# Five stretches of VectorE routing per part instead of three, among the attention slots of a cross-attention and mixture-of-experts kernel

## The reference

```
y = x + attn(layernorm(x), ctx)       # 16 heads of 16, layernorm of q and k per head, softmax over 154 keys
h = layernorm(y)
scores = sigmoid(h @ W_router)        # 8 experts
sel = top_k(scores + bias, 2)         # w = the two scores, divided by their sum
out = y + shared_ffn(h) + sum_k w_k * expert_ffn[sel_k](h)
```

## Time and profile before

| what | value |
|---|---|
| median of 3 runs | 616.65 us (615.98 to 617.1) |
| the profiled execution, its own time | 616.69 us |
| span of its trace | 614.9 us |
| busy: TensorE, VectorE, ScalarE, GpSimd | 524.6, 345.0, 239.4, 244.2 us |
| the attention slots in the trace | 52.8 to 301.6 us |
| the shared expert; the experts | to about 380 us; 404 us to the end |

### The profile page before, as it was taken

One profiled execution on the slowest core, in us unless ns is written; L12 is line 12 of the kernel. 1 busy time (PEld: TensorE's weight loads), 2 busy tenths in 40 slices (PEclk: granted clock), 3 DMA queues, 4 the chain that ended last, 5 costly groups with the idle time before them and its releaser, 6 DMA issues.

```text
span 614.9 us, 10970 instructions
## 1 busy us (share of the span) xinstructions
PE 524.6 (85%) x2868; PEld 311.6 (51%) x2869; DVE 345.0 (56%) x1040; ACT 239.4 (39%) x468; POOL 244.2 (40%) x218
## 2 busy tenths in 40 slices
PE   4746899998798977988689999479999999999990
PEld 3633245544354444433265555157676766767670
DVE  5875556777747757635556663225555555555550
ACT  0256888776647834654324111012222222222220
POOL 5353411120011533442114475605656547564644
PEclk9956999998969967988879999879999999999996
DMA  8903701110011211121054384225656547565634
GB/s 276 354 30 132 212 18 36 45 61 18 17 36 35 88 52 53 60 80 52 19 190 150 105 275 155 91 73 80 116 84 105 99 80 118 86 110 88 103 55 48
DMA packets 41685, 59.75 MB, mean 97 GB/s; under 512 B 6703, under 2 KB 32047, under 8 KB 41168
## 3 DMA queue, kind: packets, MB, share of 16 engines
q0 software_dynamic: 16256, 26.49, 21.2%
q1 hardware_dynamic: 25392, 32.82, 17.9%
HBM read 31.76 MB, written 29.52 MB: 100 GB/s over the span
## 4 chain that ended last, share of the span: by engine, by line
PE 67%; DVE 13%; DMA 7%; issue 5%; ACT 4%; POOL 2%; POOLq 1%; SPq 1%; DVEq 0%; ACTq 0%
PE bankS L955 13%; PE bankS L971 8%; PE bankV L866 7%; PE bankR L741 7%; PE bankS L1006 6%; PE bankQ L741 5%; DMA out<-VR,attn 5%; PE bankV L870 3%; PE bankS L841 2%; PE bankS L853 2%; PE bankR L748 1%; ACT attn L622 1%; PE bankS L1022 1%; PE bankD L944 1%; PE bankQ L962 1%
## 5 line engine op out<-in xcount | busy, mean ns | idle before, releaser
L530 POOL DMA_INDIRECT out<-VR,attn x72 | 111.1, 1544 | 101.2 <-DVE VR L1417 57.0
L955 PE MATMUL bankS<-experts,scores_in 128*128 x288 | 105.0, 498 | 2.1 <-issue 1.1
L473 POOL DMA_INDIRECT sorted_rows<-XR,route x64 | 63.3, 989 | 107.1 <-PE bankD L872 48.6
L622 ACT ACTIVATE attn<-bankS,bias 128x512 f32<-128x512 f32 x128 | 81.1, 680 | 24.3 <-PE bankS L841 24.2
L971 PE MATMUL bankS<-experts,scores_in 96*128 x288 | 74.3, 380 | 0.0
L866 PE MATMUL bankV<-attn,VS 128*32 128x512 f32 x256 | 69.0, 664 | 1.7 <-DVE OTT L1192 1.7
L955 PEld LDWEIGHTS bankS<-experts,scores_in 128*128 128x128 f32 x288 | 52.6, 193 | 34.2 <-issue 9.7
L868 PE MATMUL bankD<-attn,ON 128*32 128x512 f32 x256 | 68.9, 664 | 0.0
L705 ACT ACTIVATE scores_in<-bankS 128x192 f32<-128x192 f32 x72 | 23.8, 330 | 110.8 <-PE bankS L955 110.8
L409 POOL DMA_DIRECT2D x_in<-in_xT x13 | 9.6, 736 | 127.3 <-PE bankQ L741 126.3
L1402 DVE TENSOR_TENSOR scores_in<-scores_in,bankS 128x192 f32<-128x192 f32 x72 | 25.5, 354 | 52.5 <-ACT scores_in L705 52.1
(11 more groups left out here) (252 smaller groups left out, 916.9 us busy)
## 6 DMA issues: line engine op xcount, KB each, us to landing
VS<-sorted_rows SPq DMA_DIRECT2D x72, 130.0 KB, 2.9
x_cols<-X2T SPq DMA_DIRECT2D x16, 256.0 KB, 2.0
scores_in<-x_cols SPq DMA_DIRECT2D x16, 256.0 KB, 2.8
out<-X POOLq DMA_DIRECT2D x8, 512.0 KB, 4.1
x_in<-in_xT POOLq DMA_DIRECT2D x15, 256.0 KB, 3.5
experts<-in_wgu SPq DMA_DIRECT2D x2, 1536.0 KB, 9.1
X<-in_x SPq DMA_DIRECT2D x1, 2048.0 KB, 16.2
experts<-in_wd SPq DMA_DIRECT2D x2, 768.0 KB, 15.9
```

The lines of the kernel that those rows point to most:

```text
L473: pool.indirect_dma_start(sorted_rows.rearrange("s p r -> (s p) r"), bass.IndirectOffsetOnAxis(ap=index, axis=0), rows, None, bounds_check ...
L530: pool.indirect_dma_start(out, bass.IndirectOffsetOnAxis(ap=dest[:, i:i + 1], axis=0), y_out[:, i % 4], None, bounds_check=B * N + SPARE - ...
L622: act.activation(Pb[:, u % 2, c, :], bankS[:, c % GH, :], ACT.Exp, bias=bias[:, b, GH * g + c:GH * g + c + 1] if c < GH else biasR[:, b, g ...
L955: last = pe.matmul(gate_bank(k)[:, 0:2 * F], x_col[:, k, c * P:(c + 1) * P], rhs, start=(c == 0), stop=(c == KC - 1))
```

## The change

`chosen(k)` is cut in two: `best(k)` (four instructions, up to the number of the best expert) and `taken(k)` (three, and for k = 0 a fourth that strikes the expert out). `counted` is cut before the weights, six instructions that become `weights()`. No instruction is added or taken away; those of `weights` read the counts from `cum_b`, where they stood before too.

```
-            def chosen(k):
-                oh = (oh1, oh2)[k]
+            def best(k):
                 link(dve.tensor_reduce(small[:, 1], sbias, AX, ALU.max))
                 link(dve.tensor_tensor(cand, sbias, tile_of(small[:, 1]), ALU.is_equal))
                 link(dve.tensor_tensor(cand, cand, of_e(rev), ALU.mult))
                 link(dve.tensor_reduce(small[:, 2 + k], cand, AX, ALU.max))
+            def taken(k):
+                oh = (oh1, oh2)[k]
                 link(dve.tensor_tensor(oh, cand, tile_of(small[:, 2 + k]), ALU.is_equal))
...
                 dve.tensor_copy(total, a_[:, PT - 1, :]).then_inc(r_tot, 1)
-                link(dve.tensor_tensor(slot, a_, oh1, ALU.subtract))
+            def weights():
+                link(dve.tensor_tensor(slot, cum_b, oh1, ALU.subtract))
...
                         c, step = divmod(u // 2 - 8, PP)      # even slots
                         if c >= 0 and step == 0:
                             sums_of(c, bankR)
+                            weights()
+                        if c >= -1 and step == PP - 1:
+                            taken(0)
+                            best(1)
...
                         c, step = divmod(u // 2 - 6, PP)      # odd slots
                         if c >= 0 and step == 0:
                             scored(c)
-                            chosen(0)
+                            best(0)
                         if c >= 0 and step == 1:
-                            chosen(1)
+                            taken(1)
                             counted(c)
```

## The result

| what | before | after |
|---|---|---|
| median, lowest and highest | 616.88 us (615.98 to 617.37) | 598.62 us (597.61 to 602.12, 4 runs) |
| ratio, 95% interval | 1 | 0.9719 (0.9691 to 0.9747) |
| the profiled execution, its span | 616.69, 614.9 us | 598.51, 596.7 us |
| busy: TensorE, VectorE | 524.6, 345.0 us | 513.0, 344.8 us |
| mean granted clock | 0.907 | 0.933 |

The kernel before was measured again beside it, hence 616.88 and not 616.65. The change makes the kernel 2.8% faster; the profiled execution is 18.2 us shorter. The forecast was 594.6 us in a range of 589 to 608. Busy TensorE falls by 11.6 us although it executes the same instructions: that part is the clock.

What follows compares the result with a forecast made beforehand. TensorE, busiest, was taken to be bound by L748's waits for VectorE's rows and the clock falls behind them. Savings of 23.7 us, less 1.64 for one fall, left 22.1: 616.7 - 22.1 = 594.6 us, range 589 to 608.

Steps and rivals of the forecast that it cites:

- The path and its price: Slots 14 to 30 and behind the loop: TensorE's L748 pays one for one for routing at odd slots' ends.
- The price of the even slots' ends: Work moved to even slots' ends delays TensorE by 1.10 us in slots 15 and 23, 0.78 in 17 and 25.
- the count matmuls: Slots 16 and 24: two pairs of at most 0.36 us that overlap, charged at 0.4 us.
- The clock in slots 14 to 18 and 24, 25: Clock at its full level there; slots 16 and 17 take 8.28 us less, 24 and 25 4.44 less.
- The rival in which the clock falls as often as before: Only idle time counts, 9.6 us less, giving 607.1 us; chance 0.22.
- the one in which short gaps hold it down: Gaps of 0.8 to 1.9 us keep slots 14 to 18 and 22 to 25 at the lower clock: 641.8 us; chance 0.05.
- L1099 runs 1.02 us earlier and is over before: Slot 22: L1099 ends before GpSimd's addition (L455), so L748 waits 1.86 us as in slot 14.
- another instruction caught: Slot 22: if GpSimd's addition catches another instruction instead of L1099, 1.27 us come back; included in the range.
- one fall elsewhere: One clock fall after one of the two gaps of 1.86 us (slots 14 and 22), charged at 1.64 us.
- Behind the loop: L748's wait there falls from 7.32 to 4.93 us; the gain taken is 2.3 us, as the norm also needs ScalarE.
- shift with it: Stages behind the attention start on what it releases and shift with it, so its whole gain reaches the total.

Runs made afterwards that it cites:

- weights_only: Against the kernel before, only the six instructions of the weights are moved; best and taken stay as before the change. 607.94 us, ratio 0.986.
- behind_rows: Changed kernel with the three stretches at odd slots' ends put into the next even slot, behind out_rows and ahead of norm. 587.94 us, ratio 0.9563.
- scatter_later: Changed kernel with GpSimd's second sixteen scatters spread over more slots, each pair waiting two slots longer. 593.06 us, ratio 0.9611.
- again: The changed kernel, unchanged, measured a second time. 596.73 us, ratio 0.9689; its profiled execution took 603.44 us.
- bias_early: Changed kernel with GpSimd's bias addition for piece 13 put directly behind that for piece 12, ahead of four scatters. 597.62 us, ratio 0.9694.
- combined_late: Changed kernel with routing behind the rows' output, also behind the loop, scatters spread, bias additions of pieces 13, 14 and 15 moved. 583.55 us, ratio 0.9466.

## Why the prediction was right, and where it was not

**The path and its price: right.** L748 follows what stands at an odd slot's end. Forecast and measured waits of L748: 1.86 and 1.85 in slot 14, 1.14 and 0.89 in 16, 1.06 and 1.45 in 18, 1.38 and 1.87 in 24, 1.02 and 1.00 in 30, 4.93 and 5.14 behind the loop. `weights_only` shows the one for one, `behind_rows` that nothing else of any size holds L748 in slots 14 to 24.

**The price of the even slots' ends: right in 15, too high in 17.** 1.10 us forecast in slot 15, 0.52 + 0.47 = 0.99 measured. In slot 17 I charged 0.78 for the weights and 0.4 for the count matmuls, and measured 0.21 for the first. Most likely the two overlap: the count matmuls make TensorE's own next scores later, and so give VectorE the more room. The error runs on: 0.57 us less delay in 17 is 0.39 us more wait in 18. In slot 23 nothing waited; most likely TensorE was late itself, behind the 4.15 us and a fall of the clock in slot 22. No run was made to test that; `scatter_later`, where slot 22 waits 3.49 us and slot 23 runs at 1.00, has 0.40 us there. Without the delay in 23 the steps of the forecast give 1.38 + 1.10 - 0.44 = 2.04 for slot 24; measured 1.87. Slot 25 had no wait either, where 17 had 0.21.

**The clock in slots 14 to 18 and 24, 25: right.** It is 1.00. The 8.3 us forecast for slots 16 and 17 came as 9.0, the largest term. The rival in which the clock falls as often as before, 607.1 us, and the one in which short gaps hold it down, 641.8, did not come about: the six gaps of slots 14 to 18, 0.2 to 1.85 us, left the clock at its upper level, in `again` too. The swinging between the levels, of which the Trainium skill tells on the page "TensorE: Matmul & The Clock Gate", section "A second HAM failure mode: psum-queue depth-cycling", did not occur there: in these slots the trace does not bear that rule out. Elsewhere the clock did fall behind small gaps, at 273.64 before and in slot 26 of `scatter_later`.

**Slot 22: the step that failed,** 2.9 us. I wrote that "L1099 runs 1.02 us earlier and is over before". It ran earlier, but the hold begins before GpSimd's addition does in the trace: L1099 started at 205.38, 0.65 us ahead of L455, and ended only with it, at 207.35. Moving it towards the start of the hold lengthened it, 1.97 against 1.45 us; `bias_early` shows the addition to be the cause. The row of before (L1099 first, L455 0.13 us behind it, both ending together) was the sign: an instruction that began first was held all the same. The wait came out 2.29 us above the 1.86 forecast, 1.80 of it this hold, and the clock fell behind it (0.91 over 18.85 us, an estimated 1.7 us); the 1.10 us not lost in slot 23 make it 2.9. That the hold alone brought the fall is not shown: in `bias_early`, without it, the clock fell too. I had named 1.27 us for another instruction caught, but not this place and not this size.

**Slot 28: not foreseen,** 3.6 us. I left GpSimd's queue out, since the change does not touch it. The run of scatters begins 4.6 us into slot 26 before and 4.7 after, but slots 26 and 27 now take 12.54 us and not 15.81. Before, the seventh scatter waited 2.02 us for TensorE (L872); after, it and the eighth follow at once: six in a row became eight, and the run reaches into slot 28, where ScalarE's exponentials came only after it. The forecast had no term for it; `scatter_later` returns it. So this loss hangs on the gain of slots 26 and 27 below. It is not the length alone, as `behind_rows` and `combined_late` show, and the cause stays open.

**Slots 26 and 27: 3.3 us better** than forecast. The clock did not fall there, 1.00 against 0.78. In `again` these two slots take 12.54 us as well. I had left them as they were, and charged one fall elsewhere instead. This part is luck: in `scatter_later`, with the same two waits in slot 26 (0.77 and 0.75 us), the clock fell in slot 27 (0.76) and the two slots took 14.24 us. Why it falls in one execution and not in another no run tells.

**Behind the loop: the wait right, the gain given back.** The wait shrank as forecast, 7.32 to 5.14. But from that L748 to the end it took 2.5 us more. The table by stretch from that L748 on, of the kernel before:

```profile
308.91:318.32 9.41, 8.72 (x32) 7.34 (x33) 3.68 (x16) 0.60 (x1) 1.17 (x2) 0.61 0.73 225
...
327.00:333.00 6.00, 6.00 (x22) 3.04 (x22) 3.84 (x17) 3.42 (x4) 1.94 (x2) 1.00 0.59 189
```

and of the kernel after:

```profile
288.17:298.71 10.54, 9.85 (x32) 8.28 (x33) 5.07 (x24) 0.82 (x3) 1.05 (x2) 0.54 0.76 242
...
307.00:313.00 6.00, 6.00 (x14) 2.76 (x13) 3.69 (x16) 3.42 (x4) 1.05 (x2) 0.72 0.58 185
```

The lower level lasted 10.2 us in both; but before it began at 306.1, 2.8 us ahead of the wait's end, after at 287.6, 0.6 ahead. Of the longer wait more of the slow time was idle time. The same 32 matmuls take 8.72 and 9.85 us. And after, the clock fell once more for 3.4 us at 308.1, before it did not (clock 0.72 against 1.00 in the second rows). At half speed the two come to an estimated 1.1 and 1.7 us, near the 2.5. The forecast took what lies behind to "shift with it"; the clock does not shift with it. That this return is a rule, and not this execution's, no run was made to show.

**The sum.** The failed steps cost 2.9, 3.6 and 2.5 us, the clock gave 3.3 back, slots 16, 17, 24 and 25 another 1.0, and the fall that was charged without a place 1.6. The rest, 0.7 us, lies in small pieces: the 0.48 ahead of slot 14, slot 18, and what stands against them in slots 29 to 31. Forecast 22.1 less, measured 18.2. That the two are so near is in part luck: 9.0 us of losses that the sum did not hold stand against 5.9 of gains, most of them the clock's.

## What to carry to other kernels

Work that no one needs soon belongs behind the instruction on which the bottleneck engine waits; cutting it into shorter stretches gets part of this (597 to 599 us), putting it behind clears the wait (586 to 588). An instruction of an engine that is not the bottleneck can hold another engine merely by running beside it: when you shift a queue in time, lay both queues side by side again and look at what now meets, and take a hold's start to lie ahead of its row. And once waits are down to 1 or 2 us, read them in the trace, since the clock alone moves the time of one program by more.

## What the runs showed of the hardware

- GpSimd's addition (L455, 1.28 us) holds VectorE. Caught were L1099, a scalar operation of 0.17 us, for 1.97; L1236, a product of two arrays, 0.23 us, for 2.02; L1125, the same kind, 0.69 us, for 2.37; L1213, a pair of 0.74 us, for 2.39. The scatters L473 beside them held none. The Trainium skill, page "SBUF — State Buffer", section "SBUF: two separate sides", says that the port pair that the two engines share is an exclusive lock: of a GpSimd operation that reads SBUF and a VectorE one with two SBUF inputs or in a 2-port mode, whoever starts second fully blocks. The trace agrees that it blocks fully; but by the rows of L1099, L1236 and L1125 VectorE started first, by 0.13 to 0.65 us, and was the one held. So the hold begins ahead of the start that the profile gives for GpSimd.
- ScalarE's exponentials began 1.31 us after a run of eight scatters had ended, twice, and 0.72 us behind their scores where the run was broken up. They began 1.32 us after a run of six in `combined_late`, and were on time in the middle of a run of ten in `behind_rows`. Cause open.
- The clock is not a function of the waits: with nearly equal waits one program took 598.5 us at 0.933 and 603.4 at 0.925. Gaps of up to 1.9 us in slots 14 to 18 did not take it down in either profile of the changed kernel; behind the 4.15 us in slot 22 it fell in both, and slots 22 to 24 then took 28.13 or 32.90 us. It also fell behind 2.43 us in `bias_early` and behind 0.77 and 0.75 us in slot 26 of `scatter_later`, where waits as good as equal left it at 1.00 in the changed kernel.
